# A transformer block on one core: rows filled in 16 pieces, gates and modulation columns ahead of the first products

## The reference

```
mod = (silu(c) @ wmod).reshape(2, 6, 1, 256)
sa, ca, ga, sb, cb, gb = mod[:, 0], ..., mod[:, 5]
ga, gb = sign * max(abs, 0.25)
h = layernorm(x) * (1 + ca) + sa
x = x + ga * attention(h, W_qkv, b_qkv, W_out, b_out)   # 16 heads of 16, causal
h = layernorm(x) * (1 + cb) + sb
return x + gb * ffn(h, ...)        # 256 -> 1024 -> 256, relu, 3 low-rank experts of rank 8, softmax-routed
```

## Time and profile before

| | us |
|---|---|
| median of 3 runs | 1360.38 (1359.32 to 1360.94) |
| the profiled execution | 1362.05 |
| its span | 1360.2 |
| busy: PE | 1221.2 |
| busy: DVE | 950.9 |
| busy: ACT | 804.3 |
| busy: POOL | 175.7 |

### The profile page before, as it was taken

One profiled execution on the slowest core, in us unless ns is written; L12 is line 12 of the kernel. 1 busy time (PEld: TensorE's weight loads), 2 busy tenths in 40 slices (PEclk: granted clock), 3 DMA queues, 4 the chain that ended last, 5 costly groups with the idle time before them and its releaser, 6 DMA issues.

```text
span 1360.2 us, 23639 instructions
## 1 busy us (share of the span) xinstructions
PE 1221.2 (90%) x9456; PEld 714.0 (52%) x9456; DVE 950.9 (70%) x1247; ACT 804.3 (59%) x1616; POOL 175.7 (13%) x125
## 2 busy tenths in 40 slices
PE   2988889999999999999999999999962999999997
PEld 2875433444444444444444444434322888888886
DVE  7767897888787887787887777865203567666654
ACT  2542366777677777677777667777631544444442
POOL 8003700000111000000000000000003132323211
PEclk9987799999999999999999999999865999999999
DMA  4684130031041021031021021000013011111200
GB/s 154 217 267 175 40 72 10 8 84 35 31 115 47 10 77 37 10 89 40 9 62 52 10 79 49 9 9 11 9 34 123 1 62 49 42 43 55 63 16 32
DMA packets 58118, 79.53 MB, mean 58 GB/s; under 512 B 12680, under 2 KB 28752, under 8 KB 58008
## 3 DMA queue, kind: packets, MB, share of 16 engines
q1 hardware_dynamic: 58008, 78.01, 18.9%
HBM read 47.57 MB, written 29.62 MB: 57 GB/s over the span
## 4 chain that ended last, share of the span: by engine, by line
PE 66%; DVE 16%; ACT 8%; issue 7%; DMA 1%; POOL 1%; SPq 0%; POOLq 0%; ACTq 0%; DVEq 0%
PE ps L829 20%; PE ps L811 17%; PE ps L373 8%; PE ps L791 8%; ACT prob L1011 6%; PE ps L767 5%; PE ps L905 5%; DVE mx L1161 4%; DVE hid_lo L1273 4%; DVE xhat L401 2%; DVE stats L391 1%; ACT o_sb L1002 1%; DVE x L1227 1%; DVE x L1223 1%; DMA rd<-rden_rows 1%
## 5 line engine op out<-in xcount | busy, mean ns | idle before, releaser
L1011 ACT ACTIVATE prob<-ps 128x512 f32<-128x512 f32 (+3 forms) x1280 | 597.7, 535 | 258.1 <-PE ps L767 136.3
L1161 DVE TENSOR_REDUCE mx<-ps 128x2 f32<-128x1024 f32 (+1 forms) x512 | 593.2, 1190 | 171.7 <-PE ps L791 97.6
L811 PE MATMUL ps<-qst,kst 64*128 64x512 f32 (+3 forms) x1280 | 380.9, 448 | 13.1 <-ACT prob L1011 7.3
L811 PEld LDWEIGHTS ps<-qst,kst 64*128 64x128 f32 x1280 | 174.7, 186 | 323.7 <-ACT prob L1011 283.7
L829 PE MATMUL ps<-prob,vw 128*32 128x512 f32 (+3 forms) x2560 | 306.6, 551 | 9.8 <-ACT o_sb L1002 9.8
L791 PE MATMUL ps<-kst,qst 62*128 62x512 f32 (+3 forms) x1280 | 247.7, 417 | 20.9 <-DVE mx L1161 17.7
L791 PEld LDWEIGHTS ps<-kst,qst 62*128 62x128 f32 x1280 | 125.9, 191 | 64.0 <-DVE mx L1161 55.7
L767 PE MATMUL ps<-mask_kh,eye_h 64*128 64x128 bf16 x1024 | 100.6, 225 | 0.0
L829 PEld LDWEIGHTS ps<-prob,vw 128*32 128x32 f32 x2560 | 51.7, 108 | 74.6 <-ACT prob L1011 49.7
L1273 DVE TENSOR_TENSOR hid_lo<-hidf,hid_hi 128x512 fp32r<-128x512 f32 x64 | 73.1, 1182 | 12.8 <-ACT hid_hi L1055 12.7
L905 PE MATMUL ps<-w_hi,hid_hi 128*128 128x284 f32 x256 | 78.6, 328 | 2.0 <-ACT hid_hi L1055 2.0
(11 more groups left out here) (150 smaller groups left out, 1402.8 us busy)
## 6 DMA issues: line engine op xcount, KB each, us to landing
qk_parts<-parts SPq DMA_DIRECT2D x32, 512.0 KB, 4.2
qst<-qk_parts SPq DMA_DIRECT2D x192, 64.0 KB, 2.3
kst<-qk_parts SPq DMA_DIRECT2D x192, 64.0 KB, 2.3
xs<-in_x SPq DMA_DIRECT2D x16, 512.0 KB, 7.2
o_all<-o_sb SPq DMA_DIRECT2D x32, 256.0 KB
o_raw<-o_all SPq DMA_DIRECT2D x16, 256.0 KB
rd<-rden_rows SPq DMA_DIRECT2D x16, 256.0 KB
out<-y SPq DMA_DIRECT2D x8, 512.0 KB, 3.1
```

The lines of the kernel that those rows point to most:

```text
L811: last = pe.matmul(ps[:, banks[par], 0:BLK - skip], kst[g % 2][rows, pair, t * P:(t + 1) * P], qst[g % 2][rows, pair, J * BLK + skip:(J + ...
L1011: act.activation(prob[:, n % P_BUFS, h, 0:width], ps[:, L_BANK + i % L_BUFS, 0:width], ACT.Exp).then_inc(exp_done, 1)
L1161: dve.tensor_reduce(mx[:, u % 2, :, pairs[0], r, cb], ps[:, bank:bank + 2, 0:width], AX, ALU.max).then_inc(max_red, 1)
```

## The change

`clear_rows` fills each stripe in four pieces of 32x1024, one after the other by a semaphore, 16 pieces in all (`CLEARS`); SP and POOL wait for 16. The first filling also waits for `xhat_done` 2, the scaling of block 1. Both calls of `columns` and `gate_rows` go ahead of the products of block 0. The columns go to banks 7 and 6, which q and k of block 0 use later (`COL_BANK`), and the gate rows to banks 2 and 3. `project` is split into `project_qk` and `project_v`; in block 0, q is multiplied before block 1 is transposed, k and v after. On DVE statistics (`moments`) and scaling (`rescale`) are separate calls, so that the residue of block 0 can stand between those of block 1, and `silu_wide` moves ahead of the first scaling. ACT modulates block 0 before the root of block 1 and copies the gate rows right after it. Line numbers move by up to 22.

```diff
@@ clear_rows
-                    for k, (stack, r0, value) in enumerate((
-                            (kst[q], 32, 1.0), (kst[q], 96, 1.0), (qst[q], 32, 0.0), (qst[q], 96, 0.0))):
-                        until(pool, ones_set[q], k)
-                        pool.memset(stack[r0:r0 + 32].rearrange("p a t -> p (a t)").bitcast(F32),
-                                    value).then_inc(ones_set[q], 1)
+                    k = 0
+                    for stack, r0, value in ((kst[q], 32, 1.0), (kst[q], 96, 1.0), (qst[q], 32, 0.0), (qst[q], 96, 0.0)):
+                        for c in range(CLEARS // 4):
+                            until(pool, ones_set[q], k)
+                            cols = slice(c % 2 * S // 2, (c % 2 + 1) * S // 2)
+                            pool.memset(stack[r0:r0 + 32, c // 2, cols].bitcast(F32), value).then_inc(ones_set[q], 1)
+                            k += 1
...
                 pool.wait_ge(consts, 5)
+                pool.wait_ge(xhat_done, 2)
                 clear_rows(0)
-                pool.wait_ge(ones_set[0], 4)
+                pool.wait_ge(ones_set[0], CLEARS)
@@ TensorE
-                def project(n):
+                def project_qk(n, cs):
                     q = n % 2
                     pe.wait_ge(h_lo, n + 1)
-                    for c in range(2 * KC):
+                    for c in cs:
+                        if n == 0 and QK_BANK + c >= COL_BANK - 1:
+                            pe.wait_ge(mod_out, 4)
...
+                def project_v(n):
+                    q = n % 2
                     until(pe, v_out, n)
                     if n == 0:
-                        pe.wait_ge(mod_out, 2)
-                    if n == 3:
-                        gate_rows()
                         pe.wait_ge(rows_out, 2)
-                    if n == 4:
-                        columns(((2, 4), (3, 3)), V_BANK)
-                        pe.wait_ge(mod_out, 4)
...
-                columns(((0, 1), (1, 0)), V_BANK)
+                columns(((0, 1), (1, 0)), COL_BANK)
                 pe.wait_ge(consts, 4)
                 turn(0)
+                columns(((2, 4), (3, 3)), COL_BANK - 1)
+                pe.wait_ge(setup, 2 * KC)
+                gate_rows()
                 pe.wait_ge(w_lo, 2)
-                for n in range(NBLK):
+                project_qk(0, range(0, KC))
+                turn(1)
+                project_qk(0, range(KC, 2 * KC))
+                project_v(0)
+                for n in range(1, NBLK):
@@ ScalarE
-                root(1)
                 act.wait_ge(mod_out, 2)
                 modulate(0)
-                act.wait_ge(setup, 1)
+                root(1)
+                act.wait_ge(rows_done, 1)
+                for v in range(2):
+                    act.copy(gates[:, v].rearrange("p b d -> p (b d)"), ps[:, V_BANK + v, :]).then_inc(rows_out, 1)
+                act.wait_ge(setup, 2 * KC + 1)
@@ VectorE
-                normalise(0)
+                moments(0)
+                dve.wait_ge(silu_done, 1)
+                dve.wait_ge(consts, 1)
+                for k in range(KC):
+                    for b in range(B):
+                        ready(dve.tensor_scalar(silu_wide[:, k, b, :], ones[:], silu[:, k, b:b + 1], None,
+                                                ALU.mult), wait=False)
+                rescale(0)
...
-                normalise(1)
+                moments(1)
                 low(0)
...
+                rescale(1)
+                dve.wait_ge(cols_done, 2)
+                modulations((2, 3), COL_BANK - 1)
```

More of the change, by code:

```diff
@@ L154 @@
 W_STEP, W_FROM = 6, 10
+CLEARS = 16
 def until(eng, sem, count):
@@ L339, in build_program @@
              "y_done", "dve"))
-        T_BANK, V_BANK, QK_BANK = 0, 2, 4
+        T_BANK, V_BANK, QK_BANK, COL_BANK = 0, 2, 4, 7
         S_BANK, L_BANK, L_BUFS, O_BANK = 0, 4, 3, 7
@@ L426, in load_stacks @@
                     sp.wait_ge(parts_stored[n % 2], 16 * 4 * (n // 2 + 1))
-                    sp.wait_ge(ones_set[q], 4)
+                    sp.wait_ge(ones_set[q], CLEARS)
                     cols = slice(n * BLK, (n + 1) * BLK)
@@ L651, in _ @@
                 clear_rows(1)
-                pool.wait_ge(ones_set[1], 4)
+                pool.wait_ge(ones_set[1], CLEARS)
                 widen(1)
@@ L751, in _ @@
                 pe.wait_ge(wmod_in, 16)
-                columns(((0, 1), (1, 0)), V_BANK)
+                columns(((0, 1), (1, 0)), COL_BANK)
                 pe.wait_ge(consts, 4)
                 turn(0)
+                columns(((2, 4), (3, 3)), COL_BANK - 1)
+                pe.wait_ge(setup, 2 * KC)
+                gate_rows()
                 pe.wait_ge(w_lo, 2)
-                for n in range(NBLK):
+                project_qk(0, range(0, KC))
[3 more added lines that the diff above has]
+                for n in range(1, NBLK):
                     if n + 1 < NBLK:
                         turn(n + 1)
-                    project(n)
+                    project_qk(n, range(2 * KC))
+                    project_v(n)
                 def mask(banks, col, table):
@@ L989, in _ @@
                         modulate(n + 1)
-                    if n == 3:
-                        act.wait_ge(rows_done, 1)
-                        for v in range(2):
-                            act.copy(gates[:, v].rearrange("p b d -> p (b d)"), ps[:, V_BANK + v, :]).then_inc(rows_out, 1)
                     if n + 2 < NBLK:
@@ L1085, in _, with moments, rescale @@
                 link1 = Links(dve, dve1)
-                def normalise(n):
+                def moments(n):
                     dve.wait_ge(x_in[n % 2], (n // 2 + 1) * 16)
                     statistics(dve, link1, xs[:, n % 2], stats, mv, var_done)
+                def rescale(n):
                     standardise(dve, link1, n, xs[:, n % 2], mv, rstd, xhat, std_done, xhat_done, (xT_done, n * KC))
@@ L1129, in _ @@
                 dve.wait_ge(cols_done, 1)
-                modulations((0, 1), V_BANK)
+                modulations((0, 1), COL_BANK)
                 dve.wait_ge(bias_in, 32)
                 ready(dve.tensor_scalar(bq_sb[:, 0:KC], bq_sb[:, 0:KC], QSCALE, None, ALU.mult))
-                normalise(1)
+                moments(1)
                 low(0)
-                dve.wait_ge(silu_done, 1)
-                for k in range(KC):
-                    for b in range(B):
-                        ready(dve.tensor_scalar(silu_wide[:, k, b, :], ones[:], silu[:, k, b:b + 1], None,
-                                                ALU.mult), wait=False)
+                rescale(1)
+                dve.wait_ge(cols_done, 2)
+                modulations((2, 3), COL_BANK - 1)
                 for n in range(NBLK):
                     if n + 2 < NBLK:
-                        normalise(n + 2)
+                        moments(n + 2)
+                        rescale(n + 2)
                     if n + 1 < NBLK:
@@ L1145, in _ @@
                     qk_low(n)
-                    if n == 4:
-                        dve.wait_ge(cols_done, 2)
-                        modulations((2, 3), V_BANK)
                     v_rows(n)
```

## The result

| | before | with the change |
|---|---|---|
| median, us | 1360.94 of 5 runs (1359.32 to 1364.16) | 1351.06 of 5 runs (1346.00 to 1353.01) |
| the profiled execution, its span | 1362.05, 1360.2 | 1346.0, 1344.3 |
| first matmul of attention starts | 120.82 | 110.63 |
| DVE's memset of `zg`, where the last stage begins | 1013.55 | 1003.36 |
| from there to the end | 346.7 | 341.0 |

The ratio is 0.9922, with a 95% interval from 0.9901 to 0.9944: faster by 0.6 to 1.0%. Six more runs of the same kernel (last experiment) have a median of 1347.45; all eleven together 1347.5. The forecast was 1347.3. The table shows more than the total: the profiled execution gained 15.9 us of span, of which 10.2 came in the first stage, where the change is, and 10.2 stood again at the end of attention. The other 5.7 us arose in the last stage, in which no instruction was changed.

What follows compares the result with a forecast made beforehand. DVE bounds the first stage to 31 us, PE from 44, with SP's x loads just below. First stage 12.3 plus start of attention 0.8 gives 13.1 us: 1360.38 to 1347.3, forecast 1344 to 1350 (0.54), range 1339 to 1356.

Steps and rivals of the forecast that it cites:

- signs of being wrong: Trace signs against the forecast: no wait for x, a clock fall in the gaps, or pieces above 1.2 us.
- Setup: Up to block 1: scalings of block 0 in 1.38 us, block 1 starting at 36.4 instead of 44.4, gaining 8.0 us.
- The wait of the residue: DVE's residue of block 1 held beside POOL's memsets: bounds 0 and 1.0 us, 0.5 taken.
- SP's round: SP's issue cycle from x load to x load, 11.3 us against PE's 9.3, putting block 6 at 90.3.
- The first stage: Up to block 6 on PE: starting at 90.3 instead of 102.62, a gain of 12.3 us and not 19.2.
- Start of attention: POOL's second filling in pieces shortens the wait for DVE's cast of row maxima: 0.8 us, bounds 0 and 1.3.
- The clock in the gaps: Three short PE gaps in the first stage may lower the clock; a fall before block 6 costs 2.1 us.
- x falls further behind: Rival: SP's rounds take 13 instead of 11 us, costing 4, plus a 2.1 us clock fall: 1353.4; chance 0.17.
- 4.8 and 7.0 us: PE time freed by taking gate rows out of block 3 (4.8) and columns out of block 4 (7.0).
- a piece costs 2.7 us or more: Rival, slower: SP's stack loads wait for 16 pieces; 2.7 us each loses all 13 us, 3.0 gives 1364.7; chance 0.07.
- nothing arrives: Rival: reordering is real, but pieces of about 2.3 us and slow x loads add up to 1360; chance 0.06.
- x keeps pace: Rival: SP's 11 us round shrinks, block 6 starts at 83.4, time 1340.4; chance 0.16.

Runs made afterwards that it cites:

- last experiment: The changed kernel run again unaltered: median 1347.45 us of 6 runs, ratio 0.9913, first attention matmul at 114.12 us.
- x on ACT: The changed kernel with the x loads of blocks 5 to 7 issued by ACT instead of SP: median 1339.39 us, ratio 0.9849, first attention matmul at 103.43.
- the filling alone: The kernel before with only POOL's 16 late pieces, columns and gate rows left in blocks 4 and 3: median 1348.36 us, ratio 0.9922, first attention matmul at 109.73.

## Why the prediction was right, and where not

The total came out in the stated range, and the mechanism that it rests on, x at the pace of SP's queue, is the one that the runs show. The scored median, 1351.06, lies 1 us outside the 1344 to 1350 that the prediction called its forecast; the eleven runs of the change together (1347.5) lie inside. Two of its own signs of being wrong did appear: the granted clock was 0.91 and not 1.00 from 60 to 80 us, and it fell in a gap. The first stage's products ended at 109.3, not near 107. Step by step:

- **Setup.** Predicted: scalings of block 0 1.38 us, gate rows over at 23.5, scalings of block 2 over at 34.0, block 1 at 36.4. Measured: 1.38, 23.04, 33.88, 35.82. The gain is 8.6 us by the chain's 44.39 (8.3 by the timeline's 44.15) instead of 8.0.
- **The wait of the residue**, taken at 0.5 between 0 and 1.0, was 0: 1.21 us at 33.81 as at 31.37 in the earlier trace rows. This is the rule of the Trainium skill that the prediction weighed ("SBUF — State Buffer", "Who interferes with whom"): an instruction of VectorE with two SBUF inputs is held only by a GpSimd instruction that reads SBUF. This trace agrees; the rule, and not the middle of the bounds, gave the right start of block 1 (35.9). In the kernel with late whole memsets the residue ran beside a cast and a difference of POOL, which read, and took 1.41 us.
- **Pieces** at 1.0 us: measured 7.97 and 8.12 us for eight.
- **SP's round.** This is the term that was mis-sized. The stores of block 1 started at 46.16, 0.7 us earlier than predicted, and x of block 5 at 57.02, as predicted (57.3). Then the rounds were 11.77 and 11.83 us where 11.3 was taken, and the load of block 7 took 5.81 us to land where 4.74 was taken, with the DMA share at 0.98 to 1.01 from 60 to 100 us. Block 6 started at 92.18 instead of 90.3: 0.7 us from the rounds and 1.1 from the landing. The rows for this term came from a less loaded stretch: from 60 to 100 us the kernel before moved 261 GB/s at a share of 0.88, and the changed kernel 310 at 1.00.
- **The first stage** ended 10.2 us earlier instead of 12.3. What was missing is the term above, 1.9 us. The other 0.2 is no cost: the chain of before counts block 6 from the end of the transposes (102.62), while its first product starts at 102.37 in the timeline, and from there the 96 matmuls take 17.1 us in both kernels.
- **Start of attention.** 0.8 taken, measured 1.4: the cast of the maxima takes 0.80 us (2.55 in the trace of before), and the bound was 1.3.

The sum of these is 11.6 us instead of 13.1. It reads as 9.9 in the first medians and 12.9 over all runs of the change against the median of 1360.38; the changed kernel's two groups of runs have medians 3.6 us apart, so they can't tell 11.6 from 13.1. That 1347.3 and 1347.5 lie so close is luck.

The 10.2 us at the end of attention are also luck, for they are not the 10.2 of its start. Matmul by matmul the lead of the changed kernel goes from 10.2 at the start to 12.2 once the row maxima are in (188.99 before, 176.83 after; 1.4 of this is the term above). Then it falls to 11.0 (772.98 and 761.95) and to 9.7 (904.36 and 894.65), and ends at 10.2. At the first of these places the granted clock is 0.77 over 15 us (750 to 765) where it was 0.89 before (762 to 777), at the second 0.89 (885 to 900) where it was 1.00 (897 to 912). So clock falls in attention hid the gain at its start in this pair of profiles.

**The clock in the gaps** was part of the rival in which x falls further behind, and it was real, though not in each execution. In the first profile there was one fall in these blocks, from 65.5 to 69, behind a wait of PE for scaled x (1.91 us); it cost nothing, since x of the next block was late anyway. In the second profile of the same kernel it came ahead of block 6, where nothing hides it any more. Chain and timeline of PE, the change again:

```profile
81.48 5.86 DMA xs<-in_x
...
93.09 19.67 PE ps L375 x96
```
```profile
91.21 1.32 PE L729 MATMUL ps<-ident,xhat 128*128 128x128 f32 x8 [2.10 <-DVE xhat L403]
...
93.65 0.63 PE L375 MATMUL ps<-hT_lo,wqkv_hi 128*128 128x512 f32 x1
```

The matmul takes 0.63 us here and 0.40 otherwise, and the 96 matmuls 19.67 instead of 17.08. The other 0.9 us of the later stage came before: x of block 7 was issued at 81.48 instead of 80.62. The Trainium skill ("TensorE: Matmul & The Clock Gate", "HAM oscillation — how this bites in real kernels") says that bursts with waits for data between them pay for the clock again and again. The traces agree in part: PE waits for scaled x three times in each of the three profiles of this first stage, and one wait of the three was followed by the lower level (waits of 1.91, 2.10 and 1.87 us; one of 1.94 was not), at a price of up to 2.6 us. The prediction read its one fall as following 5 us without large products; by the earlier trace rows the clock was falling between 84.5 and 85 (0.72), 2 us after the last of them. With x on ACT the 20 us from 60 to 80 have no gap and the clock stays at 1.00. The forecast and this rival were therefore not exclusive: the same program runs with or without the fall that counts, and the prediction should have carried the spread of a fall (0 or 2.6 us here, 1.5 per block later) as a width of its own.

**Not asked** was one thing: what each half is worth by itself. The prediction lists 4.8 and 7.0 us as gone from blocks 3 and 4 and then lets SP's round set block 6, which is why the total held. The columns and gate rows, 11.8 us, brought 3.1 us alone and nothing on top of the filling. What they cost in the new place (8.8 us between 14.3 and 23.0, and 5.0 us of block 1's start against the filling alone) was in the prediction's working for the setup, and not set against what they freed.

The rivals in which a piece costs 2.7 us or more, or nothing arrives, are out by the row of 1.0 us. "x keeps pace" did not happen here, but its time is what the chip gave once x left SP's queue: 1339.4 against 1340.4.

## What to carry to other kernels

When two interruptions are taken off a bottleneck engine, look at which transfers they had been hiding: here the x load stood behind twelve stack loads in one queue, the queue's round (11.8 us) was longer than the engine's (9.3), and moving three load instructions to another engine's queue brought 7.2 us of stage, where the whole reordering had brought 10.2. Cut long fills into pieces rather than move them late: a piece holds the other engine for 1.0 us instead of 3.5, and then it need not be moved at all. Take a queue's pace from a stretch as loaded as it will be after the change, and measure the halves of a change against one another before crediting either.

## What the runs showed of the hardware

- A group of 24 matmuls of 28 columns, back to back at 0.11 us each and with PE shown as busy throughout, was followed by the lower clock level in up to seven of seven places, at about 1.5 us of time each. Groups of twelve and of six, with matmuls of 284 columns between, were never followed by it in the three profiles that have them. Whether a group of 24 is, changes from run to run of one program (three of seven, then seven of seven).
- Splitting the group has a price too: against the count of falls, one more group per block cost 3.6 us in all, about 0.5 us a block. Of this 2.4 us are longer waits of PE for ACT's high part, and 1.2 us PE's own busy time. Why ACT's part comes later, no run shows.
- The spread of a kernel's times (10 us in several experiments above; 2.5 us with the change and 7.0 without where the router products were spread) comes at least partly from where the clock falls. A single profile of each kernel shows one draw of it, so stages without falls have to be compared, and not whole spans.
- Beside a memset of GpSimd, a scaling of 128x256 on VectorE takes about as long as the memset: four of them took 4.1 us in all beside memsets of 1.0 us and 13.34 us beside memsets of 3.5 us, and 1.38 us alone. An instruction with two SBUF inputs was not held beside memsets (1.21 us).
